# Graph network on one core: 166 regions walked in place of 168, 625 tiles gathered in place of 628, and in the attention output TensorE takes a chunk's product ahead of the next chunk's turn

## The chip, the core and the metric

The kernel runs on one core of a Trainium2 chip. The metric is the device time of one execution in microseconds (us), as the median of several runs. A core has TensorE (PE, matrix products and transposes into PSUM; its weight loads are shown apart as PEld), VectorE (DVE), ScalarE (ACT), GpSimd (POOL) and SyncE (SP). They run at the same time and wait for each other by semaphores. TensorE's clock is granted at one of two levels, 1.2 or 2.4 GHz; the profile shows the mean grant of a stretch as a share of the upper one.

## The reference

`x` holds 5000 nodes of 128 features, `src` and `dst` name the ends of 80000 edges (sorted by `dst`). Four graph layers are added to `x` one after the other:

```python
h = relu(layernorm(x)); x = x + L0(h, edges, edge_attr_128)   # GAT with edge rows, 3 iterations
h = relu(layernorm(x)); x = x + L1(h, src, dst)               # sum of relu(x[src]) by dst, MLP, batch norm
h = relu(layernorm(x)); x = x + L2(h, edges, edge_attr_4)     # 4 steps: typed messages, sums by dst, GRU
h = relu(layernorm(x)); x = x + L3(h, src, dst)               # transformer attention over edges, batch norm, FFN
# in L0, three times:
k, v = x[src] + edge_attr through wk, wv;  alpha = sum(q[dst] * k) / sqrt(32)      # 4 heads
a = exp(alpha - segment_max(alpha, dst));  a = a / segment_sum(a, dst)
att = segment_sum(a * v, dst)
att = layernorm(att @ w_ao.T + b_ao + x)                      # the "attention output"
m = layernorm(gelu(att @ w_int.T) @ w_out.T + att);  h = gru(m, h);  x = layernorm(h)
```

## The kernel before

The edges lie in 625 **tiles** of 128 (one edge per partition), the nodes in 40 **blocks** of 128. Where a tile's edges point into several blocks, it is taken once for each: a **step** is a pair of tile and block. 625 + 40 - 1 = 664 steps are enough for any sorted `dst`. The kernel walks 672, since `STEPS = ROW_C * ROW_K` = 7 x 96; the last eight repeat tile 624 with block 40, which stands behind the nodes. Four steps are a **region** (`GROUP`), four regions a turn of a loop (`REGIONS`), so 168 regions in 42 turns (`LOOPS`). `turns` writes the first and the last turn out and loops over the rest.

The stages, in order:
- Per iteration of L0 (three): a **score pass** (`gat_score_pass`), `gat_softmax`, a **value pass** (`gat_value_pass`), the **attention output** (`attended`), the feed-forward part, the GRU and the norm. In the score pass GpSimd gathers the rows `x[src]`, one indirect DMA of 128 rows a step (`gathers_by_step`, L969, into a ring of four regions); SyncE loads the edge rows (L1369); VectorE makes selection matrices (L991), adds the edge rows (L1421) and forms the scores (L1431 to L1438); TensorE transposes (L1453, L1461) and multiplies (L1473, L1480); ScalarE copies out of PSUM, and SyncE stores the values in HBM (L1376). The value pass reads them back (L1519), GpSimd and VectorE weigh half of a region each (L1529, L1545), and TensorE sums by node block in PSUM (L1578); the number of a block's last region is read from a table (`value_done`).
- L1 has the **mixing pass** (`mixing_pass`) and L2 four **update passes** (`update_pass`). They don't walk steps: each tile is gathered once (`gathers_by_tile`, L986, into a ring of eight regions; 157 regions, `TILE_REGIONS`, the last one with tile 624 and three columns of index 0), and 196 pairs of region and block are summed. SyncE waits for a region's gathers and passes the news on (`relay_landed`, L1084, and L1087 for the last region); VectorE picks a selection three pairs ahead (L1036) and adds the sum of a pair (L1060, behind TensorE's L1074). Near the end the node chunks that are complete are transposed (L1130; L1278 in the mixing pass) and run through the gates between the pairs.
- L3 has the **transformer pass** (`transformer_pass`), again 168 regions of steps with gathers at L969, then attention output, norms and feed-forward.

In `attended` the nodes lie in ten chunks of 512 columns. GpSimd forms the sums with the bias for chunk c (L1960, L1963, once chunk c-2 has been turned); VectorE weighs them (`weigh`, L1970); TensorE transposes (`turn`, L1998); ScalarE copies (L2021); TensorE takes the product with `w_ao` (`project`, L2004); VectorE adds (`finish`, L1975); then TensorE transposes again (L714) for the norm, VectorE takes the statistics (L729), ScalarE scales, TensorE turns back (L722). Each engine's order is written out by hand: VectorE in turn t does `weigh(t)`, `finish(t-1)`, `measure(t-2)`, `scale(t-3)`; TensorE `turn(t)`, `project(t-1)`, `turn_nodes(t-2)`, `turn_back(t-4)`.

## Time and profile before

| | before |
|---|---|
| runs, us | 9507.3, 9508.18, 9516.57; median 9508.18 |
| profiled execution, us | 9523.01 (its span 9521.2) |
| mean granted clock of TensorE | 0.787 |
| busy us: PE / PEld / DVE / ACT / POOL | 6133.9 / 4836.9 / 4478.9 / 2035.6 / 6058.3 |
| instructions | 134262 |

Busy shares are means over stages with different limits, and idle time costs only where the engine is waited for. The first score pass runs from about 173 to 1025 us, its value pass from 1072 to 1274, the attention output to about 1336; the mixing pass starts at 4283, the four update passes at 5171, 6003, 6840 and 7672, the transformer pass at 8557.

### The profile page before, as it was taken

How to read it: one execution, taken by the hardware profiler on the slowest of the kernel's cores; microseconds unless marked ns; L12 is line 12 of the kernel's file. 1: busy time of each engine (PE TensorE's matmuls, PEld its weight loads, DVE VectorE, ACT ScalarE, POOL GpSimd, SP SyncE). 2: the span in 40 equal slices, each digit the busy share in tenths (PEclk: the TensorE clock that was granted, in tenths of full speed). 3: DMA queues.
4: the chain of work that ended last, by engine and by line, in shares of the span. 5: the costliest groups of instructions: out<-in, count | busy, mean ns of one | idle time of the engine just before them, and what ended most of it. 6: DMA issues, size and time to landing. Idle time of an engine off the chain costs nothing. (4 is left out here: it accounts for less than half of the span.)

```text
span 9521.2 us, 134262 instructions
## 1 busy us (share of the span) xinstructions
PE 6133.9 (64%) x31445; PEld 4836.9 (51%) x31446; DVE 4478.9 (47%) x9847; ACT 2035.6 (21%) x4047; POOL 6058.3 (64%) x6482
## 2 busy tenths in 40 slices
PE   4878787887787886874445446544644654476666
PEld 3666655666646665743443444344344434445554
DVE  5555755555845556842224223322422332257776
ACT  2444244444054443160001000000100000021112
POOL 2777435777417775517774777677677767747773
PEclk7999899999889998985556557655855765598888
DMA  3555523555604554602112222222222222233332
GB/s 87 159 159 159 156 79 98 159 159 155 184 11 143 159 159 121 181 23 53 53 53 78 53 52 78 61 53 53 86 53 52 78 61 53 52 97 105 105 105 65
DMA packets 708452, 916.20 MB, mean 96 GB/s; under 512 B 148175, under 2 KB 448091, under 8 KB 708078
## 3 DMA queue, kind: packets, MB, share of 16 engines
q0 software_dynamic: 198368, 429.61, 17.3%
q1 hardware_dynamic: 487108, 441.09, 14.8%
q10 hardware_dynamic: 22730, 42.81, 1.2%
q8 instruction: 83, 1.36, 0.1%
q14 instruction: 163, 1.34, 0.0%
HBM read 702.69 MB, written 210.24 MB: 96 GB/s over the span
## 5 line engine op out<-in xcount | busy, mean ns | idle before, releaser
L986 POOL DMA_INDIRECT states<-table_typed,tile_idx x2512 | 2401.7, 956 | 993.6 <-issue 767.7
L969 POOL DMA_INDIRECT states<-table_x,src_idx x2016 | 1910.3, 948 | 722.4 <-issue 599.5
L1074 PE MATMUL psum<-states,select 128*128 x4480 | 1003.7, 400 | 1118.1 <-DVE t L1060 1037.5
L1074 PEld LDWEIGHTS psum<-states,select 128*128 128x128 f32 x4480 | 893.2, 298 | 1253.9 <-issue 1253.5
L1036 DVE SCALAR_TENSOR_TENSOR select<-dst_all,pair_start,psum 128x512 f32<-128x512 f32 x476 | 355.4, 747 | 1583.8 <-SPq L1084 1323.7
L1473 PE MATMUL psum<-wt,l_scores_mixT 128*128 128x256 f32 x4032 | 992.8, 389 | 38.2 <-issue 35.5
L1074 PE MATMUL psum<-states,l_update_select 128*128 x2688 | 570.8, 385 | 538.3 <-DVE t L1060 538.3
L1480 PE MATMUL psum<-t,l_scores_spread 128*128 x4032 | 586.1, 288 | 443.1 <-DVE score L1438 440.4
L969 POOL DMA_INDIRECT l_pass_ring<-table_kv,src_idx x672 | 642.9, 957 | 297.7 <-issue 204.6
L1473 PEld LDWEIGHTS psum<-wt,l_scores_mixT 128*128 128x128 f32 x4032 | 728.1, 190 | 194.9 <-issue 106.8
L1074 PEld LDWEIGHTS psum<-states,l_update_select 128*128 128x128 f32 x2688 | 510.7, 285 | 611.5 <-issue 611.5
L1421 DVE TENSOR_TENSOR states<-states 128x512 f32<-128x512 f32 x504 | 349.1, 693 | 975.0 <-DMA states<-table_x,src_idx 975.0
L1480 PEld LDWEIGHTS psum<-t,l_scores_spread 128*128 128x128 f32 x4032 | 490.7, 190 | 559.8 <-issue 559.8
L991 DVE TENSOR_TENSOR select<-psum,dst_local 128x512 f32<-128x512 f32 x1008 | 692.4, 687 | 125.9 <-PE psum L1578 48.7
L986 POOL DMA_INDIRECT states<-table_x,tile_idx x628 | 594.0, 946 | 232.8 <-issue 176.2
L1222 ACT COPY t<-psum 128x512 f32<-128x512 f32 x40 | 23.5, 586 | 2793.4 <-PE psum L1130 2793.4
L1529 POOL TENSOR_TENSOR t<-t,score 128x264 f32<-128x264 f32 x504 | 345.2, 688 | 417.3 <-DMA t<-rows_dram 412.6
L1578 PE MATMUL psum<-t,select 128*128 128x132 f32 x4032 | 492.4, 281 | 73.1 <-DVE t L1545 40.5
L1036 DVE SCALAR_TENSOR_TENSOR l_update_select<-dst_all,pair_start,psum 128x512 f32<-128x512 f32 x264 | 197.0, 746 | 717.3 <-SPq L1084 680.0
L1578 PEld LDWEIGHTS psum<-t,select 128*128 128x128 f32 x4032 | 469.0, 192 | 100.6 <-issue 100.6
L1389 ACT COPY l_scores_spread<-psum 128x512 f32<-128x512 f32 x504 | 295.4, 586 | 732.3 <-PE psum L1453 732.3
L1401 ACT COPY w<-psum 128x512 f32<-128x512 f32 x504 | 295.5, 586 | 712.2 <-PE psum L1473 623.6
(414 smaller groups left out, 9618.1 us busy)
## 6 DMA issues: line engine op xcount, KB each, us to landing
rows_dram<-l_scores_values SPq DMA_DIRECT2D x504, 264.0 KB
t<-rows_dram SPq DMA_DIRECT2D x504, 264.0 KB, 3.0
states<-in_edge_attr_dram SPq DMA_DIRECT2D x2016, 64.0 KB
states<-table_typed,tile_idx POOLq DMA_INDIRECT x2512
table_typed<-states ACTq DMA_DIRECT2D x36, 1024.0 KB, 4.5
states<-table_x,src_idx POOLq DMA_INDIRECT x2016
table_x<-select SPq DMA_DIRECT2D x50, 256.0 KB, 2.3
l_pass_ring<-table_kv,src_idx POOLq DMA_INDIRECT x672
```

The lines of the kernel that those rows point to most:

```text
L969: pool.indirect_dma_start(out=ring[:, k % REGIONS, u, :], out_offset=None, in_=table, in_offset=at).then_inc(gathered[k % REGIONS], 16)
L986: pool.indirect_dma_start(out=ring[:, k % TILE_RING, u, :], out_offset=None, in_=table, in_offset=at).then_inc(gathered[k % REGIONS], 16)
L991: eng.tensor_tensor(select[:, r, lo:lo + n, :], numbers.unsqueeze(1).broadcast_to([P, n, P]), dst_local[:, bass.ds(step_of(i, r, lo), n)]. ...
L1036: dve.scalar_tensor_tensor(out=picked(more, k), in0=dst_all[:, bass.ds(column, GROUP)].unsqueeze(2).broadcast_to([P, GROUP, P]), scalar=pa ...
L1074: ins = pe.matmul(psum[:, k % 2, 0:P], picked(more, k)[:, u, :], slots[:, bass.ds(at[u], D)], start=u == 0, stop=u == GROUP - 1)
L1389: act.copy(spread[:, r % 2, :, :], bank4(psum[:, 0, :])).then_inc(p_spread, 1)
L1401: act.copy(in_pairs(key[:, r % 2, :, :]), made(r)[:, :, :, 0:D]).then_inc(p_evacuated, 1)
L1421: dve.tensor_tensor(ring[:, r, :, :], ring[:, r, :, :], attr[:, r, :, :], ALU.add).then_inc(p_mixed, 1)
L1473: ins = pe.matmul(made(r)[:, u // pair, u % pair, :], mixT[:, r % 2, u, :], both, start=True, stop=True)
L1480: ins = pe.matmul(queries[:, u // pair, u % pair, :], spread[:, r % 2, u, :], q, start=True, stop=True)
L1529: pool.tensor_tensor(ring[:, room(half, r), SHARE:, :].rearrange("p u (h e) -> p u h e", h=GAT_HEADS), ring[:, room(half, r), SHARE:, :].r ...
L1578: ins = pe.matmul(to, select[:, r, u, :], ring[:, room(half, r), u, :], start=False, stop=True, skip_group_check=True)
```

## The change

Three edits. (1) The passes over steps walk 166 regions, `EDGE_REGIONS`, in place of 168: the last turn has two regions and the one ahead of it is written out too, `regions_of` and `led` stop at the last region, counts of semaphores follow (`STEP_COUNTS`, `step_landed`), and the eight steps of `score` that are no longer written are set to zero. (2) The last region of the passes over tiles gathers one tile in place of four. (3) In `attended` TensorE's `project(t-1)` stands ahead of `turn(t)`.

```diff
+EDGE_REGIONS = -(-(TILES + BLOCKS - 1) // GROUP)
...
-                    link(dve.tensor_scalar(counts_i[:], psum[0:1, 7, CHUNK - VALUE_BANKS:], float(GROUP - 1), None, ALU.add))
+                    link(dve.tensor_scalar(counts_i[:], psum[0:1, 7, CHUNK - VALUE_BANKS:], float(GROUP - 1), float(EDGE_REGIONS * GROUP),
+                                           ALU.add, ALU.min))
...
             body(0)
-            with eng.Fori(1, LOOPS - 1) as i:
+            with eng.Fori(1, LOOPS - 2) as i:
                 body(i)
+            body(LOOPS - 2)
             body(LOOPS - 1)
...
+        def regions_of(i):
+
+            return range(min(REGIONS, EDGE_REGIONS - i * REGIONS)) if isinstance(i, int) else range(REGIONS)
+
...
-            return None if isinstance(i2, int) and i2 >= LOOPS else (i2, r2)
+            return None if isinstance(i2, int) and i2 * REGIONS + r2 >= EDGE_REGIONS else (i2, r2)
...
-        ROWS = LOOPS * GROUP * 16
-
-        TILE_COUNTS = [len(range(r, TILE_REGIONS, REGIONS)) * GROUP * 16 for r in range(REGIONS)]
...
+        STEP_COUNTS = [len(range(r, EDGE_REGIONS, REGIONS)) * GROUP * 16 for r in range(REGIONS)]
+
+        TILE_COUNTS = [len(range(r, TILES, REGIONS * GROUP)) * 16 for r in range(REGIONS * GROUP)]
+        TILE_COUNTS = [sum(TILE_COUNTS[r * GROUP:(r + 1) * GROUP]) for r in range(REGIONS)]
...
+        def step_landed(i, r, base):
+
+            return base[r] + STEP_COUNTS[r] if isinstance(i, int) and i == LOOPS - 1 else landed(i, base[r])
...
-            for k in range(STEPS // GROUP):
+            for k in range(EDGE_REGIONS):
...
-                for u in range(GROUP):
+                for u in range(min(GROUP, TILES - k * GROUP)):
...
-                sp.wait_ge(gathered[r], landed(TILE_REGIONS // REGIONS, base[r]))
+                sp.wait_ge(gathered[r], base[r] + TILE_COUNTS[r])
...
-                            for r in range(REGIONS):
+                            for r in regions_of(i):
...
+                        dve.memset(score[:, EDGE_REGIONS * GROUP:, :], 0.0)
+
...
-                            dve.wait_ge(gathered[r], landed(i, base[r]))
+                            dve.wait_ge(gathered[r], step_landed(i, r, base))
...
-                        add_blocks(dve, sums, LOOPS - 1, REGIONS - 1, W, blocks_of(dve, LOOPS - 1, REGIONS - 1))
+                        final = (EDGE_REGIONS - 1) // REGIONS, (EDGE_REGIONS - 1) % REGIONS
+                        add_blocks(dve, sums, *final, W, blocks_of(dve, *final))
...
                         for t in range(CHUNKS + 4):
+                            if 1 <= t <= CHUNKS:
+                                project(t - 1)
                             if t < CHUNKS:
                                 turn(t)
-                            if 1 <= t <= CHUNKS:
-                                project(t - 1)
```

The line `for r in regions_of(i)` takes the place of `for r in range(REGIONS)` in every body of the score, value and transformer passes.

TensorE in `attended`, from its start; before (L1998 `turn`, L2004 `project`, L714 `turn_nodes`, L722 `turn_back`):

```order
L1998 MATMUL psum<-ident,w 128x128 x8
L2004 MATMUL psum<-select,wt 128x512
L1998 MATMUL psum<-ident,w 128x128 x4
L2004 MATMUL psum<-select,wt 128x512
L714 MATMUL psum<-ident,t 128x128 x4
L1998 MATMUL psum<-ident,w 128x128 x4
L2004 MATMUL psum<-select,wt 128x512
L714 MATMUL psum<-ident,t 128x128 x4
```

The same place in the changed kernel, whose lines are numbered L2015, L2021, L728 and L736:

```order
L2015 MATMUL psum<-ident,w 128x128 x4
L2021 MATMUL psum<-select,wt 128x512
L2015 MATMUL psum<-ident,w 128x128 x4
L2021 MATMUL psum<-select,wt 128x512
L2015 MATMUL psum<-ident,w 128x128 x4
L728 MATMUL psum<-ident,t 128x128 x4
L2021 MATMUL psum<-select,wt 128x512
L2015 MATMUL psum<-ident,w 128x128 x4
```

The two sets of turning transposes at the start (x8) are parted by the first product, and each later product has moved from behind a set of transposes to ahead of it.

GpSimd at the end of the last update pass and through the transformer pass, before (L986 gathers by tile, L969 by step):

```order
L986 DMA states<-table_typed,tile_idx 128x128 x12
L977 REGISTER_ALU
L986 DMA states<-table_typed,tile_idx 128x128 x4
L93 UNCONDITIONAL_BRANCH
L2346 REGISTER_ALU
L2346 COMPARE_AND_BRANCH
L1607 UNCONDITIONAL_BRANCH
L969 DMA l_pass_ring<-table_kv,src_idx 128x256 x672
```

And in the changed kernel (L1000 and L983):

```order
L1000 DMA states<-table_typed,tile_idx 128x128 x12
L991 REGISTER_ALU
L1000 DMA states<-table_typed,tile_idx 128x128
L94 UNCONDITIONAL_BRANCH
L2363 REGISTER_ALU
L2363 COMPARE_AND_BRANCH
L1623 UNCONDITIONAL_BRANCH
L983 DMA l_pass_ring<-table_kv,src_idx 128x256 x664
```

The last region has one gather where it had four, and the pass over steps has 664 where it had 672. In the score pass the same row counts 664 too.

## Rows read from the trace of the kernel before

**Rows 1.** Windows: us; busy (xcount) of PE, PEld, DVE, ACT, POOL; PEclk; DMA share; GB/s.
```profile
500.00:600.00 100.00, 79.98 (x481) 65.64 (x481) 56.65 (x100) 42.98 (x80) 75.60 (x81) 1.00 0.55 159
...
1100.00:1200.00 100.00, 86.03 (x716) 81.86 (x715) 94.39 (x179) 7.62 (x14) 61.76 (x90) 1.00 0.80 242
...
1273.50:1325.00 51.50, 30.57 (x120) 19.08 (x120) 28.78 (x101) 21.59 (x50) 23.09 (x20) 0.77 0.00 0
```
**Rows 2.** Timeline, first score pass: first and last of 672 gathers, first softmax transposes.
```profile
172.68 0.98 POOL L969 DMA_INDIRECT states<-table_x,src_idx  x1 [89.33 <-POOLq L93]
...
1013.19 0.95 POOL L969 DMA_INDIRECT states<-table_x,src_idx  x1 [0.30 <-issue]
...
1024.95 4.94 PE L1739 MATMUL psum<-ident,score 128*96 128x128 f32 x28 [2.56 <-PEq L93]
```
**Rows 3.** Timeline, engine PE: last two bursts of the first value pass.
```profile
1265.42 3.86 PE L1578 MATMUL psum<-t,select 128*128 128x132 f32 x32 [0.55 <-DVE t L1545]
...
1269.60 3.86 PE L1578 MATMUL psum<-t,select 128*128 128x132 f32 x32 [0.32 <-DVE select L991]
```
**Rows 4.** Timeline, engine POOL: last gather of the transformer pass.
```profile
9403.38 0.95 POOL L969 DMA_INDIRECT l_pass_ring<-table_kv,src_idx  x1 [0.31 <-issue]
```
**Rows 5.** Timeline, end of the fourth update pass.
```profile
8462.83 0.95 POOL L986 DMA_INDIRECT states<-table_typed,tile_idx  x1 [0.30 <-issue]
...
8467.29 1.05 PE L1074 MATMUL psum<-states,select 128*128 x8
...
8469.56 0.75 DVE L1036 SCALAR_TENSOR_TENSOR l_update_select<-dst_all,pair_start,iota_row 128x512 f32<-128x512 f32 x1 [5.01 <-SPq L1087]
...
8470.57 0.66 PE L1130 MATMUL psum<-ident,t 128*128 128x128 f32 x4 [2.23 <-DVE t L1060]
```
**Rows 6.** Timeline: the same transposes in mixing and update passes one to three.
```profile
5072.81 1.12 PE L1278 MATMUL psum<-ident,t 128*128 128x128 f32 x4 [4.28 <-DVE t L1060]
...
5968.85 0.66 PE L1130 MATMUL psum<-ident,t 128*128 128x128 f32 x4 [1.61 <-DVE t L1060]
...
6802.17 0.66 PE L1130 MATMUL psum<-ident,t 128*128 128x128 f32 x4 [1.96 <-DVE t L1060]
...
7637.13 0.66 PE L1130 MATMUL psum<-ident,t 128*128 128x128 f32 x4 [1.73 <-DVE t L1060]
```
**Rows 7.** Timeline, attention output, first iteration: weighing of chunk 1; one whole turn.
```profile
1279.05 1.55 DVE L1970 TENSOR_TENSOR w<-w,l_attention_den 128x512 f32<-128x512 f32 x1 [1.08 <-POOL w L1963]
...
1309.45 0.69 DVE L1970 TENSOR_TENSOR w<-w,l_attention_den 128x512 f32<-128x512 f32 x1
...
1310.20 0.66 PE L1998 MATMUL psum<-ident,w 128*128 128x128 f32 x4 [1.41 <-DVE w L1970]
...
1310.69 1.02 PE L2004 MATMUL psum<-select,wt 128*128 128x512 f32 x2
...
1311.62 0.60 ACT L2021 COPY select<-psum 128x512 f32<-128x512 f32 x1
...
1311.76 0.75 DVE L1975 SCALAR_TENSOR_TENSOR t<-psum,vec,states 128x512 f32<-128x512 f32 x1 [1.61 <-PE psum L2004]
...
1312.10 1.18 POOL L1963 TENSOR_TENSOR w<-w,states 128x512 f32<-128x512 f32 x1
...
1312.42 0.88 DVE L729 BATCH_NORM_STATS2 norm_stat<-psum 128x6 f32<-128x128 f32 x4
...
1313.89 0.69 DVE L1970 TENSOR_TENSOR w<-w,l_attention_den 128x512 f32<-128x512 f32 x1
```
**Rows 8.** Timeline, engine PE, attention output: a turn at the lower clock.
```profile
1319.31 1.11 PE L1998 MATMUL psum<-ident,w 128*128 128x128 f32 x4 [1.40 <-DVE w L1970]
...
1321.92 1.03 PE L714 MATMUL psum<-ident,t 128*128 128x128 f32 x4
```
**Rows 9.** Timeline: GpSimd and VectorE at the head of the attention output.
```profile
1276.35 1.07 POOL L1960 TENSOR_TENSOR w<-states,bv_rows 128x512 f32<-128x512 f32 x1
...
1276.53 1.44 DVE L1970 TENSOR_TENSOR w<-w,l_attention_den 128x512 f32<-128x512 f32 x1
```

More of the change, by code:

```diff
@@ L1381, in _ @@
                         for r in range(REGIONS):
-                            sp.wait_ge(p_out[r], 16 * LOOPS)
+                            sp.wait_ge(p_out[r], 16 * len(range(r, EDGE_REGIONS, REGIONS)))
                     @b.scalar
@@ L1395, in body @@
                         def body(i):
-                            for r in range(REGIONS):
+                            for r in regions_of(i):
                                 if nxt := led(i, r, 1):
@@ L1423, in body @@
                         def body(i):
-                            for r in range(REGIONS):
+                            for r in regions_of(i):
                                 if nxt := led(i, r):
@@ L1464, in body @@
                         def body(i):
-                            for r in range(REGIONS):
+                            for r in regions_of(i):
                                 j = region_of(i, r)
@@ L1516, in body @@
                     def body(a, i, half):
-                        for r in range(REGIONS):
+                        for r in regions_of(i):
                             at_least(sp, p_summed, region_of(i, r) - (ROOMS - 1))
@@ L1525, in body @@
                     def body(a, i, half):
-                        for r in range(REGIONS):
+                        for r in regions_of(i):
                             weights = score[:, bass.ds(step_of(i, r), GROUP), :]
@@ L1538, in body @@
                     def body(a, i, half):
-                        for r in range(REGIONS):
+                        for r in regions_of(i):
                             j = region_of(i, r)
@@ L1568, in body @@
                         plan = by_step(pe, value_row, region_of(i, 0) * (GROUP + 1), REGIONS * (GROUP + 1), BANKS_USED * CHUNK)
-                        for r in range(REGIONS):
+                        for r in regions_of(i):
                             j = region_of(i, r)
@@ L1617, in body @@
                         def body(i):
-                            for r in range(REGIONS):
+                            for r in regions_of(i):
                                 act.wait_ge(p_scored, region_of(i, r) + 1)
@@ L1634, in body @@
                             blocks = blocks_behind(dve, i)
-                            for r in range(REGIONS):
+                            for r in regions_of(i):
                                 j = region_of(i, r)
@@ L1638, in body @@
                                 dve.wait_ge(p_projected, j + 1)
-                                dve.wait_ge(gathered[r], landed(i, base[r]))
+                                dve.wait_ge(gathered[r], step_landed(i, r, base))
                                 dve.tensor_tensor(prod, ring[:, r, :, 0:D], bank4(q_bank(r)), ALU.mult).then_inc(p_multiplied, 1)
@@ L1692, in body @@
                         def body(i):
-                            for r in range(REGIONS):
+                            for r in regions_of(i):
                                 if nxt := led(i, r, 1):
@@ L2317, in program @@
         with nc.Fori(0, GAT_ITERS) as it:
-            gat_score_pass("l0_scores", [it * ROWS] * REGIONS)
+            gat_score_pass("l0_scores", [it * n for n in STEP_COUNTS])
             gat_softmax("l0_softmax")
@@ L2329, in program @@
         node_rows("l1_norm", resT, hT, LN_EPS, plus=xT)
-        mixing_pass("l1_sums", table_x[:], [GAT_ITERS * ROWS] * REGIONS, hT, t1, wt[:, GIN1, :], wcol("1_b1"))
+        mixing_pass("l1_sums", table_x[:], [GAT_ITERS * n for n in STEP_COUNTS], hT, t1, wt[:, GIN1, :], wcol("1_b1"))
         batch_norm("l1_second", t1, wcol("1_gamma"), wcol("1_beta"), residual=resT, weight=wt[:, GIN2, :], bias=wcol("1_b2"))
@@ L2348, in program @@
                 update_pass(f"l2_update{k}", table_typed[k].ap().rearrange("n (t f) -> (n t) f", f=D),
-                            [GAT_ITERS * ROWS + n * (1 + k) + it * (2 * n) for n in TILE_COUNTS], hT,
+                            [GAT_ITERS * m + n * (1 + k) + it * (2 * n) for m, n in zip(STEP_COUNTS, TILE_COUNTS)], hT,
                             parts_of(wt, GGIH, 3), parts_of(wt, GGHH, 3), gate_bias[:, 1, :], wcol("2_b_ih", 2), wcol("2_b_hh", 2),
@@ L2355, in program @@
         projected_rows("l3_norm", resT, xT, LN_EPS, w3[:, 0:3, :].rearrange("p a b -> p (a b)"), 3 * D, table_kv, plus=hT, query_width=D)
-        transformer_pass("l3_pass", [GAT_ITERS * ROWS + (1 + L2_STEPS) * n for n in TILE_COUNTS])
+        transformer_pass("l3_pass", [GAT_ITERS * m + (1 + L2_STEPS) * n for m, n in zip(STEP_COUNTS, TILE_COUNTS)])
         from_rows("l3_attention", t1, heads=L3_HEADS, eps=1e-6, weight=w3[:, 3, :], bias=wcol("3_bo"), residual=xT)
```

1 line of the change is left out of this document (added).

## The prediction, made before the changed kernel had run

> **What bounds the kernel now.** I read the windows first, 100 us apart over the span. In a score pass GpSimd is busy 75.6 us of 100 with 81 instructions, and the clock granted to TensorE is 1.00 (its upper level, 2.4 GHz) [rows 1]. The timeline says what the other quarter is: a gather takes 0.95 us and the next one starts 0.30 us later, with "issue" as the reason. From the first gather to the last of the first score pass there are 671 intervals in 840.51 us, 1.253 us each [rows 2]. So a region (4 gathers) costs 5.01 us, and the reader is to see that nothing but GpSimd's own issue stands before the gathers. The same rhythm fills the transformer pass and the mixing and update passes [rows 4, 5]. In a value pass no gather runs; VectorE is busy 94 us of 100 and the DMA engines 0.80 [rows 1], and TensorE sums four regions in bursts that start 4.18 us apart [rows 3]. The attention output is bound by none of its engines: TensorE 30.6, VectorE 28.8, ScalarE 21.6 and GpSimd 23.1 us of 51.5 [rows 1]. It is a round trip between VectorE and TensorE.
>
> **Two regions fewer in each score pass.** POOL issues 664 gathers in place of 672. The last gather starts at 1013.19 and the softmax begins at 1024.95 [rows 2]: those 11.8 us are the drain of the last regions through VectorE, TensorE, ScalarE and the store of the values, and they hang on the last region, whichever it is. 8 x 1.253 = 10.0 us less per pass, **30.1 us** in three. I cost four things at nothing. The turn that is now written out ahead of the last one runs the same instructions as in the loop. The wait values are constants. The limit on the counts is one more scalar of the same instruction. The zeroing of 8 steps of `score` stands ahead of VectorE's wait for ScalarE's copies and for region 0, whose four gathers alone take 5 us; without that cover it costs less than the 0.69 us of a 512-column operation [rows 7], 2 us in three passes.
>
> **Two regions fewer in each value pass.** The last turn has two regions, so TensorE's last burst of 3.86 us [rows 3] is half as long: 1.93 us, and ScalarE drains the last bank behind it as before. **5.8 us** in three passes. The bounds are close: 2.1 us per pass by the burst's spacing, and nothing if the last burst has to wait for its rows from HBM.
>
> **Two regions fewer in the transformer pass.** The gathers go on to its end at the same distance [rows 4]: **10.0 us**.
>
> **Three gathers fewer in the last region of the mixing pass and of four update passes.** The last region now lands after one gather, 3 x 1.25 = 3.8 us earlier at least. But how much of it arrives? At the end of the fourth update pass VectorE has waited 5.01 us for that region when it makes its selection at 8469.56 [rows 5]. The addition behind it needs also the sum of an earlier pair, which TensorE starts at 8467.29 and ends at 8468.34. Without the wait for the region that sum becomes the last thing to come. TensorE's transposes, which wait for the addition, stand idle 2.23 us before 8470.57; when they follow a sum directly this handover needs about 0.35 us (0.28 of addition and the signal; 8469.56 to 8470.57 is 1.01 with the 0.7 us selection ahead of it). So 1.9 us of the 3.8 arrive. The other update passes have 1.61, 1.96 and 1.73 us in the same place [rows 6], less 0.35 each: together **6.2 us** for the four. In the mixing pass there is no gate work between, and the idle time is 4.28 us: **3.9 us**. The bounds: nothing below what the transposes show, at most the whole wait of 5.01 us in each of five passes, 25 us.
>
> **Attention output: the product ahead of the turn.** In a turn t at the upper clock [rows 7]: the weighing of chunk t at 1309.45, TensorE's transposes of it at 1310.20 (0.75 later), the product of chunk t-1 at 1310.69 (0.49), VectorE's addition to it at 1311.76 (1.07), the statistics of chunk t-2 at 1312.42 (0.66), the next weighing at 1313.89 (1.47): 4.44 us. The product is in the middle of the chain although its input is long ready: ScalarE's copy for the next product ends at 1312.22, 2.77 us after the weighing. After the change the product of chunk t runs from about 2.8 to 3.8 us after weighing t, while VectorE does statistics; it is over before the next weighing. Queued behind its wait are the transposes of the next turn; as the copy comes first, nothing there is late. What is left of the chain is 0.75 + 0.49 + 0.65 (transposes of chunk t-2, as long as the 0.66 of the others) + 1.47 = 3.36 us. The next limit is GpSimd. Its second operation starts 2.65 us after the weighing and ends at 3.83 [rows 7], later than 3.36. At the head of the pass a weighing beside a GpSimd operation took 1.44 in place of 0.69 us: it started at 1276.53 and ended 0.55 us after GpSimd's had ended at 1277.42 [rows 9]. A weighing that waits in this way ends at 3.83 + 0.55 = 4.38, not 3.36 + 0.69 = 4.05: the turn becomes 3.69 us.
>
> The Trainium skill (SBUF — State Buffer, Who interferes with whom) says that a VectorE operation with two inputs in SBUF and a GpSimd operation that reads SBUF exclude each other for a whole instruction. By that rule the turn is 3.69 us and by a chain without it 3.36; the trace agrees with the rule at this one place.
>
> At the lower clock (1.2 GHz; the same transposes take 1.11 us) transposes and product take 2.61 us [rows 8], so the old chain is 0.75 + 2.61 + 1.03 + 1.5 = 5.9 us. In the new one TensorE itself is full: 2.61 + 2 x 0.86 for the two other sets of transposes (1.03 to 1.11 us each [rows 8], of which some 0.2 overlap with what follows) = 4.33 us. The seven turns from 1279.05 to 1313.89 took 4.98 us each [rows 7], so about 0.37 of them are slow ones (granted clock 0.77 over the stretch [rows 1]). New mean: 0.63 x 3.69 + 0.37 x 4.33 = 3.93; 1.05 us less, nine turns, three iterations: **28 us**. The bounds are nothing (another engine takes the slack) and 27 x (4.98 - 3.36) = 44 us.
>
> **Sum.** 30.1 + 5.8 + 10.0 + 6.2 + 3.9 + 28 = 84 us. The profiled execution took 9523.0 us (span 9521.2 and 1.8 around it) and becomes 9439; it lay 14.8 us above the median of the runs, 9508.2, and the same 84 us from that give **9424 us**.
>
> **Rivals.**
> A, the forecast: chance 0.62.
> B, the reordering gives nothing, because GpSimd, VectorE and ScalarE meet in every turn: 84 - 28 = 56 us, 9452. For it speaks the 1.44 us weighing [rows 9]; against it, that no engine is busy more than 0.6 of the stretch [rows 1]. Chance 0.17.
> C, everything gives its upper bound: the weighing isn't held (44) and the whole wait for the last region goes (25): 30 + 6 + 10 + 25 + 44 = 115 us, 9393. Against it stands TensorE's sum at 8468.34 [rows 5]. Chance 0.08 for most of it.
> D, the dropped regions were hidden in part, because the end of a score pass hangs on the edge rows or on the store of the values and not on the gathers: half of the 46 us of regions, 9447 with the rest. Against it: the gathers show no wait but issue [rows 2]. Chance 0.08.
> E, slower. The written-out turn makes code of two loops longer, and leaving the loop stalls every engine for fetching it. The nearest row is TensorE's 2.56 us before the first work of a new block [rows 2]: four passes of it would be 10 us, 9434, still faster. It decides only from 84 / 4 = 21 us per pass, more than the 15 us that three regions of gathers run ahead, so it would also have to stop the gathers. Chance 0.02 for slower, 0.03 for a gain eaten down to within 0.2%.
>
 The trace of before shows no stall there that reaches the gathers, since their mean of 1.253 us [rows 2] takes in the loops' end.
>
> **Numbers.** A change under 0.2% (19 us) can't be told from none here. A, B, C and D are faster by more than that: 0.95; same 0.03; slower 0.02. The range reaches to B and D with some room above, and half way to C: 9402 to 9460. A alone would be 9412 to 9436.
>
> **What would show it.** Right, if the gathers of a score pass number 664 and the softmax still starts 11.8 us after the last; if the selection at the end of an update pass no longer waits 5 us and the transposes' idle time is near 0.35; if weighings in the attention output stand 3.7 us apart at the upper clock. Wrong, if the drain has grown, if weighings last over 1 us throughout or their distance stays at 4.4, or if TensorE pauses where the loops end.

## The result and the profile after

The changed kernel takes 9420.97 us (median of 4 runs, 9416.41 to 9422.73); the kernel before took 9507.74 beside it (4 runs). The ratio is 0.9905, 95% interval 0.9893 to 0.9916: 86.8 us less, where I had said 84. The profiled execution took 9419.24 us.

The page of the changed kernel: its span, and the first row of busy times.

```profile
span 9417.4 us, 133392 instructions
...
PE 6101.1 (65%) x31213; PEld 4812.4 (51%) x31214; DVE 4442.9 (47%) x9788; ACT 2021.3 (21%) x4017; POOL 6001.4 (64%) x6429
```

The same three stretches as [rows 1] in windows (busy time of PE, PEld, DVE, ACT, POOL, granted clock, DMA share, GB/s); the third is the attention output, which now starts 12 us earlier.

```profile
500.00:600.00 100.00, 80.65 (x484) 65.88 (x482) 56.91 (x101) 42.99 (x80) 75.59 (x80) 1.00 0.54 160
...
1100.00:1200.00 100.00, 86.79 (x723) 82.60 (x722) 92.67 (x181) 7.03 (x13) 62.78 (x90) 1.00 0.82 242
...
1262.00:1313.00 51.00, 29.59 (x141) 17.78 (x142) 34.06 (x123) 30.88 (x71) 23.26 (x20) 0.89 0.00 1
```

The middle of a score pass and of a value pass is what it was. In the attention output VectorE is busy 34.1 us of 51 instead of 28.8 of 51.5, since its turns stand closer and the window reaches further past the last weighing (15 us, where it was 6). TensorE was granted 0.89 of its upper clock (2.4 GHz) instead of 0.77 in this first iteration.

The timeline of the first score pass: first and last gather, first transposes of the softmax. Then TensorE's last burst of the first value pass, and the last gather of the transformer pass.

```profile
172.72 0.97 POOL L983 DMA_INDIRECT states<-table_x,src_idx  x1 [89.79 <-POOLq L94]
...
1001.91 0.95 POOL L983 DMA_INDIRECT states<-table_x,src_idx  x1 [0.30 <-issue]
...
1014.85 1.50 PE L1756 MATMUL psum<-ident,score 128*96 128x128 f32 x6 [2.80 <-PEq L94]
...
1258.83 2.06 PE L1594 MATMUL psum<-t,select 128*128 128x132 f32 x16 [0.42 <-issue]
...
9298.96 0.95 POOL L983 DMA_INDIRECT l_pass_ring<-table_kv,src_idx  x1 [0.30 <-issue]
```

664 gathers start within 829.19 us, 1.2507 us apart ([rows 2]: 672 in 840.51, 1.2526 apart). The softmax starts 12.9 us after the last one; it was 11.8. The last burst of the value pass has 16 sums in 2.06 us, where [rows 3] shows 32 in 3.86.

The end of the fourth update pass: last gather (GpSimd), selection for the last region (VectorE), TensorE's last sum ahead of the transposes and the transposes.

```profile
8369.23 0.94 POOL L1000 DMA_INDIRECT states<-table_typed,tile_idx  x1 [0.30 <-issue]
...
8374.75 0.75 DVE L1050 SCALAR_TENSOR_TENSOR l_update_select<-dst_all,pair_start,iota_row 128x512 f32<-128x512 f32 x1
...
8377.57 1.05 PE L1088 MATMUL psum<-states,select 128*128 x8
...
8378.46 0.60 PE L1144 MATMUL psum<-ident,t 128*128 128x128 f32 x4
```

In [rows 5] the selection had waited 5.01 us and the transposes 2.23. Now neither row has an idle time: the region is there before VectorE asks for it, and TensorE goes from its sum straight into the transposes.

A turn of the attention output at the upper clock, sorted by start time.

```profile
1288.19 1.07 POOL L1977 TENSOR_TENSOR w<-states,bv_rows 128x512 f32<-128x512 f32 x1 [1.41 <-PE psum L2015]
...
1289.34 1.18 POOL L1980 TENSOR_TENSOR w<-w,states 128x512 f32<-128x512 f32 x1
...
1289.62 1.05 PE L2021 MATMUL psum<-select,wt 128*128 128x512 f32 x2
...
1289.98 0.56 DVE L755 SCALAR_TENSOR_TENSOR norm_offset<-norm_moment,norm_std 128x4 f32<-128x4 f32 x1
...
1290.46 0.68 DVE L1987 TENSOR_TENSOR w<-w,l_attention_den 128x512 f32<-128x512 f32 x1
...
1291.06 0.74 DVE L1992 SCALAR_TENSOR_TENSOR t<-psum,vec,states 128x512 f32<-128x512 f32 x1
...
1291.20 0.66 PE L2015 MATMUL psum<-ident,w 128*128 128x128 f32 x4 [0.54 <-DVE w L1987]
...
1291.69 0.60 PE L728 MATMUL psum<-ident,t 128*128 128x128 f32 x4
...
1292.33 0.89 DVE L743 BATCH_NORM_STATS2 norm_stat<-psum 128x6 f32<-128x128 f32 x4 [0.53 <-PE psum L728]
...
1294.20 0.68 DVE L1987 TENSOR_TENSOR w<-w,l_attention_den 128x512 f32<-128x512 f32 x1
```

The product (L2021) stands ahead of the weighing now, and the weighings are 3.74 us apart (1290.46, 1294.20), against 4.44 in [rows 7] and 3.69 in the prediction. But look at the row above the weighing. The norm's offset (L755), 512 numbers in all, takes 0.56 us. It ends at 1290.54, and GpSimd's second operation ends at 1290.52. The weighing itself takes its bare 0.68. The hold that I had placed on the weighing has fallen on the small operation in front of it. The experiments on this are the second half of the next section.

### The profile page after: what moved, and what is told of

The parts are those of the page before. It is cut to its first block and busy times, and to the rows that moved or that the text cites. A ratio compares the mean times of both kernels' runs of the same rounds, so it can differ in the third digit from the quotient of the medians.

```text
span 9417.4 us, 133392 instructions
## 1 busy us (share of the span) xinstructions
PE 6101.1 (65%) x31213; PEld 4812.4 (51%) x31214; DVE 4442.9 (47%) x9788; ACT 2021.3 (21%) x4017; POOL 6001.4 (64%) x6429
## 3 DMA queue, kind: packets, MB, share of 16 engines
q1 hardware_dynamic: 481924, 436.27, 14.8%
## 5 line engine op out<-in xcount | busy, mean ns | idle before, releaser
L1000 POOL DMA_INDIRECT states<-table_typed,tile_idx x2500 | 2384.5, 954 | 993.5 <-issue 761.7
L983 POOL DMA_INDIRECT states<-table_x,src_idx x1992 | 1883.9, 946 | 713.7 <-issue 587.0
L983 POOL DMA_INDIRECT l_pass_ring<-table_kv,src_idx x664 | 634.1, 955 | 295.6 <-issue 201.6
L1000 POOL DMA_INDIRECT states<-table_x,tile_idx x625 | 589.8, 944 | 231.6 <-issue 178.0
L1594 PE MATMUL psum<-t,select 128*128 128x132 f32 x3984 | 486.3, 281 | 72.1 <-DVE t L1561 40.8
```

Of the source, the lines that this page charges most:

```text
L983: pool.indirect_dma_start(out=ring[:, k % REGIONS, u, :], out_offset=None, in_=table, in_offset=at).then_inc(gathered[k % REGIONS], 16)
L1000: pool.indirect_dma_start(out=ring[:, k % TILE_RING, u, :], out_offset=None, in_=table, in_offset=at).then_inc(gathered[k % REGIONS], 16)
L1594: ins = pe.matmul(to, select[:, r, u, :], ring[:, room(half, r), u, :], start=False, stop=True, skip_group_check=True)
```

## Where the time came from, by the two traces

Both traces give marks on GpSimd: its gathers, and its first operation of each block. In us, sums over all passes of a kind:

| stretch | before | after | difference | predicted |
|---|---|---|---|---|
| three score passes, first to last gather | 2521.5 | 2487.3 | -34.2 | -30.1 |
| last gather to the value pass | 187.2 | 191.1 | +3.9 | 0 |
| three value passes | 593.9 | 588.3 | -5.6 | -5.8 |
| attention output and the block behind it | 648.8 | 614.3 | -34.5 | -28 |
| five passes by tile, first to last gather | 3946.9 | 3920.4 | -26.5 | |
| what lies behind them until the next gathers | 326.7 | 331.3 | +4.6 | |
| the two rows together | | | -21.9 | -10.1 |
| transformer pass, first to last gather | 846.5 | 835.1 | -11.4 | -10.0 |

That is 103.7 us, as much as the two profiled executions differ (9523.0 and 9419.2), but 17 more than the medians. The surplus has a place. All gather stretches together lost 72.1 us; 47 gathers fewer at 1.255 us are 59.0. The other 13.1 us is 5,781 remaining gathers that stand 0.0023 us closer on average. That is a property of the execution and not of the change: two kernels with 166 regions have 1.2526 and 1.2525 us in the first pass again (the regions alone, and the first try against the hold, both below), and the profiled execution of before had been 14.8 us above its median. Taken off, the parts are 26 (score passes with their drains), 6, 34, 14 (tiles) and 10 us: 90 for the 87 measured.

## The experiments

The experiments are built on either kernel with one addition, a register operation behind each table entry that a later wait uses. Two kernels that hold only that addition are the controls.

```
 regs = [eng.alloc_register(...) for _ in range(n)]
 eng.load(regs, table[0:1, bass.ds(first, n)])
+for k in waited:
+    held = eng.alloc_register(...)
+    eng.reg_alu(held, regs[k], max(bottom, 1), ALU.max)
+    regs[k] = held
```

> The kernel before, with one register operation (the larger of the entry and 1) behind every table entry that a later wait uses; nothing else is changed. It is the control of the kernels that are built on the kernel before. The operation stands on GpSimd's path of issues in six passes of gathers by tile, some 145 times in each, and on VectorE, TensorE and ScalarE beside them, where gathers set the pace. If it is as cheap as the gaps of 0.02 to 0.05 us between gathers allow, the five passes by tile grow by less than 1 us each and the time stays within 0.1% of 9507.7 us. If each costs GpSimd 0.05 us in the open, the passes grow by 7 us each, some 36 us in all. Whatever it is, the experiments are read against this control and not against the kernel before.

> The changed kernel with the same register operations. It is the control of the kernels that are built on the changed kernel. Against the first control it should be 87 us faster (the two kernels without these operations stood at 9420.97 and 9507.74 us), so 0.990 to 0.992 of it, whatever the operations cost.

Measured: 11389.54 us and 11293.24 us, beside 11371.47 for the kernel before, ratios 1.0016 (1.0007 to 1.0026) and 0.9922 (0.9908 to 0.9935). This chip ran every kernel 20% slower than the others did, the kernel before too, so its times are compared with one another only. A window of the first control in a score pass, to be held against [rows 1], and a row of the waits there:

```profile
500.00:600.00 100.00, 70.09 (x364) 59.80 (x363) 41.00 (x73) 31.47 (x60) 58.24 (x61) 0.86 0.41 120
...
DVE states L1436 <- issue: 51.7, 14, 6.7
```

GpSimd issues 61 gathers in 100 us instead of 81. VectorE waited there 14 times for nothing that the profile shows, up to 6.7 us each and 51.7 us in all. Why this chip does that stayed open. The second control was run again on an ordinary chip.

> The second control once more, as the base of the three kernels beside it. Its ratio to the kernel before should again be near 0.992, and in its trace the turn of the attention output 3.75 us, with the small operation of VectorE (the norm's offset, 0.16 us by itself) held to 0.55 us.

Measured: 9442.74 us beside 9512.56, ratio 0.9927 (0.9913 to 0.9940). The addition costs 0.16 to 0.22%, 15 to 21 us, more than expected. The gathers kept their distance, so it isn't on GpSimd's path of issues. By the marks of the table above, most of it lies in the value passes: they take 199.7 to 200.3 us each in this run, where the changed kernel had 195.7 to 196.5, so 12 us in three. In every kernel with the addition a value pass takes 199.7 to 202.6 us. There the addition stands four times in each turn of TensorE's loop; that it costs on that path is argued from the place and not tested. Where the other 3 to 9 us lie wasn't settled. What follows is read against the controls, and by marks in the traces.

### The reordering alone

```
 for t in range(CHUNKS + 4):
+    if 1 <= t <= CHUNKS:
+        project(t - 1)
     if t < CHUNKS:
         turn(t)
-    if 1 <= t <= CHUNKS:
-        project(t - 1)
```

> The first control with the reordering of TensorE in the attention output alone; 168 regions and 628 gathered tiles as before. My forecast: attended falls by 28 us over three executions; the trace of the changed kernel showed 34 us less between the start of that block and the next norm, so 28 to 35 us below the first control, and no other mark moves. Rival (the reordering gives nothing, since GpSimd's two operations and the transposes close the turn): within 5 us of the first control, the 34 us belonging to the shorter score accumulators or to another clock behind shorter passes.

Measured: 11354.18 us against 11389.54 of the first control, 35 us less (ratios to the kernel before 0.9981 and 1.0016). Two consecutive weighings late in the third iteration, first control and then this kernel:

```profile
4919.45 0.68 DVE L1976 TENSOR_TENSOR w<-w,l_attention_den 128x512 f32<-128x512 f32 x1
...
4923.89 0.68 DVE L1976 TENSOR_TENSOR w<-w,l_attention_den 128x512 f32<-128x512 f32 x1
```

```profile
4877.79 0.68 DVE L1976 TENSOR_TENSOR w<-w,l_attention_den 128x512 f32<-128x512 f32 x1
...
4881.54 0.68 DVE L1976 TENSOR_TENSOR w<-w,l_attention_den 128x512 f32<-128x512 f32 x1
```

4.44 us became 3.75, and from VectorE's reciprocal at the head of the attention output to GpSimd's first operation of the block behind it the three iterations lost 10.6, 9.9 and 10.5 us: 31 us in all. Rival B, by which the reordering gives nothing, is out.

### The regions alone

The changed kernel with TensorE's old order and all 628 tiles.

> The changed kernel with 166 regions, but with TensorE's old order in the attention output and with all 628 tiles gathered. By my sum: score passes 30.1, value passes 5.8 and the transformer's pass 10.0 us, so 46 us below the first control; each pass by step loses the eight gathers of two regions, 8 times 1.25 us. By the ledger of the two traces where GpSimd's gathers set the pace (34.2, 5.6 and 11.4 us) it is 51. Rival D (what is dropped was partly hidden, since something other than the gathers ends a pass): 23 us. On a chip where the passes by step run at 1120 us instead of 840, a region costs more than four gathers and the two dropped ones should give 3 times 2 times 6.7 us in the score passes, 40 us, and 55 to 60 in all.

Measured: 9491.06 us beside 9523.72, ratio 0.9964 (0.9950 to 0.9978); with the controls' 0.16 to 0.22% taken off, 48 to 54 us. In its trace the score passes take 830.50, 831.12 and 830.81 us from first to last gather, 29.1 us less than before in sum, and the transformer pass 836.67, 9.8 less. In this execution the gathers stand as far apart as before (1.2526 us in the first pass), so here the price of dropped regions can be read directly: 9.7 us per score pass on average and 9.8 in the transformer pass, for two regions each, where the prediction had 10.0. The value passes take 600.66 us in sum; the kernel with real rows below, on the same chip and with the addition too, has 605.93: 5.3 us less for a predicted 5.8. Rival D, half of it hidden, is out.

### The tiles alone

```
-for u in range(GROUP):
+for u in range(min(GROUP, TILES - k * GROUP)):
```

> The first control with the last region of a pass by tile gathered for its one real tile (625 gathers instead of 628) and nothing else. By my sum of the prediction: the mixing pass and four update passes together lose 10 us (3.9 and 4 times 1.5), of a bound of 25. By the ledger of the two traces they lost 22 us (7.3 and 14.6), of which the three gathers themselves are 3 times 1.25 us in each of five passes, 18.8 us. Theory of the issue: 18 to 22 us below the first control, the landing of the last region now some 1.8 us behind its gather. Rival (part of the 22 us came from elsewhere, as the regions' count or the clock): 10 us or less.

Measured: 11380.68 us, 9 us below the first control, on the slow chip, where the eleven runs of this kernel lie up to 40 us apart. The intervals of the two ratios (0.9996 to 1.0015 and 1.0007 to 1.0026) overlap, so this run doesn't tell 10 from 20 us. Nor does its trace: the five passes and what lies behind them take 4922 us, and the other three kernels on this chip have 4938 and 4935 with 628 gathers and 4939 with 625. So no run on record isolates the three gathers; what they bring is counted from the marks of the kernels on the other chips, in the point by point below.

### Where the last region's lateness came from

```
-at = bass.IndirectOffsetOnAxis(ap=tile_idx[:, k * GROUP + u:k * GROUP + u + 1], axis=0)
+n = k * GROUP + u if k * GROUP + u < TILES else k * GROUP + u - GROUP
+at = bass.IndirectOffsetOnAxis(ap=tile_idx[:, n:n + 1], axis=0)
```

> The first control, in which the three padding tiles of the last region of a pass by tile fetch the rows of three real tiles instead of row 0 128 times each; their sums are multiplied by zero as before. It asks why the last region landed 5.8 us behind its last gather where others took 1.8. Theory of the equal rows (128 fetches of one row go to one place of the memory and are served one behind the other): the last region lands within 2 us of its last gather, and each of the five passes by tile ends 3 to 4 us sooner. Rival (the end of the queue itself is late, whatever is fetched): the selection still waits 5 us and nothing moves. My terms for the tiles (3.9 and 6.2 us) left this out; the ledger had 7.3 and 14.6.

Measured: 9528.53 us beside 9523.72 (ratio 1.0003, 0.9994 to 1.0012). The last gather of the fourth update pass and the selection for its region:

```profile
8466.17 0.94 POOL L988 DMA_INDIRECT states<-table_typed,tile_idx  x1 [0.30 <-issue]
...
8469.78 0.75 DVE L1042 SCALAR_TENSOR_TENSOR l_update_select<-dst_all,pair_start,iota_row 128x512 f32<-128x512 f32 x1 [0.74 <-SPq L1093]
```

The selection comes 3.6 us after the last gather and has waited 0.74 us; in [rows 5] it came 6.7 us after it and had waited 5.01. In the mixing pass it comes 2.7 us after it, not 4.3. By the DMA packets of the gathers' queue, the last one ends 2.1 to 4.3 us after the last gather in the five passes, where it had been 3.7 to 6.2. So three gathers that fetch one and the same row 128 times each land 1.5 to 3.1 us later than three that fetch different rows. Around the end of the gathers the packets took 0.27 to 0.42 us each on average in the kernel before, and 0.12 to 0.13 here. In the update passes 1 MB of other transfers runs beside the last gathers, but in both kernels alike. This half of the theory holds.

The other half, that each pass then ends 3 to 4 us sooner, comes out in part. From the last gather to the next pass the five stretches are 320.2 us in sum. The kernel before had 326.7, but it lacks the addition; the two kernels that have the addition, this chip and the equal rows (regions alone, written-out turn) had 329.0 and 330.9. That is 9 to 11 us less, some 2 us a pass. The ratio says the same less sharply: 1.0003 against the first control's 1.0016 is 12 us less, though the two intervals overlap a little. TensorE's own sums are next, as the prediction had argued from 8467.29.

### The written-out turn alone

```
 with eng.Fori(1, LOOPS - 2) as i:      # was LOOPS - 1
     body(i)
+body(LOOPS - 2)
 body(LOOPS - 1)
```

> The first control with one more turn of each loop of regions written out behind the loop (the turn before the last), still 168 regions, 628 tiles and the old order. Forecast: nothing, within 3 us of the first control (0.03%). Rival E (the code behind the loop's exit is fetched late, once more per pass): 2.56 us by the nearest row in each of the four passes by step, 10 us more, and over 21 us in each pass if it were to turn the change into a loss. In the trace the stretch from the last loop turn's gathers to the end of a pass would be longer by that.

Measured: 9535.98 us beside 9523.72 (ratio 1.0012, 1.0003 to 1.0021), less than the addition costs by itself, so in total time the turn can't be seen. In the trace it can. From the last gather of a score pass to the softmax it takes 13.8, 13.6 and 13.6 us; before 11.8, 11.7 and 11.9. Two of its rows, the softmax's first transposes in the first pass and, near the end of the second, the addition for a region that came late:

```profile
1025.51 0.84 PE L1746 MATMUL psum<-ident,score 128*96 128x128 f32 x3 [4.55 <-PEq L93]
...
2364.00 0.69 DVE L1427 TENSOR_TENSOR states<-states 128x512 f32<-128x512 f32 x1 [4.22 <-DMA states<-table_x,src_idx]
```

In the first pass TensorE waits 4.55 us at the block's start where [rows 2] shows 2.56. In the second that wait is 2.94, but VectorE has waited 4.22 us for a gathered region; the waits of this kind before were 2.4 us at most in the last 20 us of that pass. On the ordinary chips the distance was 11.6 to 11.9 us in the six score passes of kernels without the written-out turn; in the 21 passes of the seven kernels with it and 166 regions it was 11.6 to 13.9, 12.4 on average. So the written-out turn has a price, as rival E said: 0.6 us per pass on average (1.9 with 168 regions), where its own estimate was 2.56. The prediction had put it at nothing. That it is a price for fetching code isn't shown. Why it shows in some passes and not in others wasn't found.

### The hold

The changed kernel's turn is 3.74 us though VectorE still waits 0.5 us in it (from 1291.80 to 1292.33, for the transposes of L728). The first try was to take that wait away.

```
 if 1 <= t <= CHUNKS:
     project(t - 1)
+if 2 <= t < CHUNKS + 2:
+    pe.wait_ge(a_done, t - 1)
+    turn_nodes(pe, t1, t - 2, first=FIRST)
 if t < CHUNKS:
     turn(t)
-if 2 <= t < CHUNKS + 2:
-    pe.wait_ge(a_done, t - 1)
-    turn_nodes(pe, t1, t - 2, first=FIRST)
```

> The changed kernel with one more move of the same kind: in the attention output TensorE takes the transposes for the statistics of chunk t-2, which are ready since the turn before, ahead of chunk t's turn instead of behind it. In the trace of the changed kernel VectorE waits 0.52 us for them in each turn of 3.75 us. If that wait goes and nothing takes its place, a turn falls to 3.35 us or less (that is what the last turn without GpSimd took), 0.4 us in each of 8 turns in 3 executions: 10 us below the second control. Rival (ScalarE, with 3.00 us of work and 0.80 us of waits for VectorE's small operations in a turn, is the next bound, or the transposes for the chunk now come later and GpSimd with them): within 3 us of the second control.

Measured: 9450.04 us beside 9523.72, ratio 0.9921 (0.9907 to 0.9935), the second control's. A turn of it:

```profile
1292.25 0.60 PE L728 MATMUL psum<-ident,t 128*128 128x128 f32 x4
...
1292.95 0.66 PE L2021 MATMUL psum<-ident,w 128*128 128x128 f32 x4
...
1293.48 0.87 DVE L743 BATCH_NORM_STATS2 norm_stat<-psum 128x6 f32<-128x128 f32 x4
...
1293.68 1.07 POOL L1983 TENSOR_TENSOR w<-states,bv_rows 128x512 f32<-128x512 f32 x1 [1.41 <-PE psum L2021]
...
1294.84 1.18 POOL L1986 TENSOR_TENSOR w<-w,states 128x512 f32<-128x512 f32 x1
...
1294.86 1.17 DVE L755 SCALAR_TENSOR_TENSOR norm_offset<-norm_moment,norm_std 128x4 f32<-128x4 f32 x1
...
1295.96 0.68 DVE L1993 TENSOR_TENSOR w<-w,l_attention_den 128x512 f32<-128x512 f32 x1
```

VectorE no longer waits: its statistics (L743) follow the addition at once. The turn is 3.75 us nevertheless, and the offset (L755) takes 1.17 us instead of 0.56. It starts at 1294.86 and ends at 1296.03; GpSimd's addition ends at 1296.02. All the time that the move had freed went into the hold. So there is a ring: GpSimd's two operations 2.34 us (1293.68 to 1296.02), the weighing that can only end after them 0.67 until TensorE's transposes start, and the transposes, on which GpSimd waits for its next chunk, 0.74 with the signal. That is 3.75 us, however early VectorE comes to the offset. The forecast of 10 us less was wrong; the rival had the outcome, not the cause.

Two theories for the ring were put against each other. Three rooms in place of two (`third` is a new tile; GpSimd waits for `a_turned` one chunk further back):

```
+def sums(c):
+    return pair[:, c % S, :, :] if c % S < V else third[:]
-at_least(pool, a_turned, c - (V - 1))
+at_least(pool, a_turned, c - (S - 1))      # S = V + 1
```

> The second control with three rooms instead of two for GpSimd's sums in the attention output, so that GpSimd runs a chunk further ahead of VectorE's weighing. The run before it showed that with VectorE's wait gone a turn is still 3.75 us, and that is GpSimd's two operations (2.33), the weighing (0.75) and the transposes (0.67) end to end. Two theories for what closes this ring. If it is the held operation (VectorE can't end an operation with both inputs in SBUF while GpSimd's runs, and GpSimd starts at the end of a turn's transposes), a third room changes nothing: 3.75 us, within 3 us of the control. If it is the rooms (a weighing waits for sums that came late), the ring opens: 3.35 us, 10 us less.

and behind that one more wait for GpSimd, which makes it start at the end of a weighing:

```
 at_least(pool, a_turned, c - (S - 1))
+at_least(pool, a_rows, c - 1)
```

> The kernel with the third room, where GpSimd also waits for the weighing of two chunks before, and so starts at the end of each weighing and no longer at the end of the transposes, 0.8 us earlier against VectorE's work. By the held operation's theory GpSimd's 2.33 us then end before the norm's offset begins (0.27 us before it by the rows of the changed kernel), the offset takes 0.16 us again and a turn 3.35 us: 0.4 us less in 8 turns of 3 executions, 10 us below the control. By the theory of the rooms it is as the third room alone or slower by the added wait.

Measured: the third room 9446.25 us, ratio 0.9928 (0.9915 to 0.9942), the control's 9442.74 within its spread. With the added wait 9434.12 us, ratio 0.9917 (0.9903 to 0.9930): by the medians 8.6 us less than the control. Third room, then the added wait:

```profile
1294.11 1.18 POOL L1991 TENSOR_TENSOR w<-w,states 128x512 f32<-128x512 f32 x1
...
1294.75 0.56 DVE L755 SCALAR_TENSOR_TENSOR norm_offset<-norm_moment,norm_std 128x4 f32<-128x4 f32 x1
...
1295.23 0.68 DVE L1998 TENSOR_TENSOR w<-w,l_attention_den 128x512 f32<-128x512 f32 x1
```

```profile
1292.52 0.68 DVE L1999 TENSOR_TENSOR w<-w,l_attention_den 128x512 f32<-128x512 f32 x1
...
1294.51 1.18 POOL L1992 TENSOR_TENSOR l_attention_third<-l_attention_third,states 128x512 f32<-128x512 f32 x1
...
1295.79 0.16 DVE L755 SCALAR_TENSOR_TENSOR norm_offset<-norm_moment,norm_std 128x4 f32<-128x4 f32 x1
...
1295.87 0.68 DVE L1999 TENSOR_TENSOR w<-w,l_attention_den 128x512 f32<-128x512 f32 x1
```

In the first the offset is held to 0.56 us, until GpSimd's end at 1295.29, and the weighings stay 3.75 us apart: the rooms are not what closes the ring. In the second GpSimd is done at 1295.69, 0.10 us before the offset begins. The offset takes 0.16 us and the weighings stand 3.35 us apart (1292.52, 1295.87), in the last six intervals of the second iteration as well (3.32 to 3.36). In the three iterations together the attention output and the block behind it take 606.9 us, where the control has 612.4 and the third room alone 612.0. So the added wait shortened this stretch by 5 us. For the whole kernel the gain is less sure: its five runs (9432.55 to 9435.38) lie below all five of the third room, but one run of the control took 9426.36, and the intervals of the ratios overlap.

> The kernel with the third room and the start behind the weighing, and TensorE's transposes for the statistics first. VectorE's own work of a turn is then 3.0 us in a row and ScalarE's 3.0 us. By the held operation's theory GpSimd ends some 0.3 us into where the offset would begin, so a turn is 3.3 us, about what the late start's removal gives alone, and the time 10 to 12 us below the control. If holds don't matter it would reach 3.05 us, 17 us below.

Measured: 9434.47 us, ratio 0.9913 (0.9899 to 0.9926), 8.3 us below the control, where 10 to 12 or 17 were expected. The offset and the next weighings in its trace:

```profile
1292.23 0.68 DVE L1999 TENSOR_TENSOR w<-w,l_attention_den 128x512 f32<-128x512 f32 x1
...
1295.16 0.25 DVE L755 SCALAR_TENSOR_TENSOR norm_offset<-norm_moment,norm_std 128x4 f32<-128x4 f32 x1
...
1295.33 0.68 DVE L1999 TENSOR_TENSOR l_attention_third<-l_attention_third,l_attention_den 128x512 f32<-128x512 f32 x1
```

The turn is 3.10 us, close to the 3.05 that stood for "holds don't matter" and below my 3.3: GpSimd, too, starts earlier within the turn, and the hold that is left is 0.09 us (0.25 instead of 0.16). Between the first and the last weighing the three iterations take 4.9 us less than with the old order, but the totals of the two kernels are equal, their runs overlapping (9425.13 to 9435.46 and 9432.55 to 9435.38). All these kernels carry the addition of the controls, and none of their ratios lies below the changed kernel's 0.9905. That the wait would help the changed kernel itself is inferred from the control and was not run.

## Why the prediction was right, point by point

- **Score passes.** The price of a region is GpSimd's issue: 29.1 us measured with regions alone, 30.1 predicted. The step "the written-out turn at nothing" was off, but by little. The stretch from the last gathers to the value passes grew by 3.9 us in the changed kernel's trace (187.2 to 191.1); over the seven kernels with 166 regions it is 187.6 to 191.1, 189.1 on average, where before and the one with real rows have 187.2 and 188.6. So 1 to 2 of the 3.9 us are the change's.
- **Value passes.** 5.6 us for 5.8, and 5.3 with regions alone. The last burst of TensorE is half as long, 1.8 us less.
- **Transformer pass.** 9.8 us with regions alone for 10.0.
- **Passes by tile.** Predicted 10.1, found 10 to 14. The pair of traces has 14 (18.8 for the 15 gathers less 4.6 given back behind them). The kernels with the addition give less: behind the gathers two of them with 628 gathers have 329.0 and 330.9 us, five with 625 have 335.2 to 340.9, 338.9 on average, so 9 are given back and 10 are left. I had measured at the transposes of [rows 5, 6] and taken their idle time as what arrives. In the pair it came out there: no wait at the selection (0.37 us in the mixing pass), no idle time at the transposes. In the mixing pass the transposes come 9.0 us after the first gather of the last region before and 4.5 after, 4.5 us for my 3.9; in the update passes 11.1, 11.4, 10.9 and 11.5 before and 9.3, 9.1, 11.8 and 9.2 after, 5.4 us in sum for my 6.2 (6.1 before rounding). That is 9.9 at these marks for 10.1. It is partly luck: in the 20 update passes of the five kernels with the addition the transposes come 9.4 to 13.2 us after that gather, 11.4 on average, so one pair of traces doesn't fix this term within a few us.
- **Attention output.** Predicted 28, found 34.5 by the traces and 31 by the reordering alone. The turn at the upper clock: 3.74 for 3.69. The mean over nine turns: 4.71 before and 3.81 after, so 0.90 us each and 24 us, not 1.05 and 28; I had taken the mean before, 4.98, from seven turns that hold the slow ones. The rest came behind the last weighing, 171.5 us per iteration before and 168.0 after, which I hadn't counted. In the reordering alone the 31 us divide into 27.4 between first and last weighing and 3.6 behind (169.3 against 170.5 per iteration). So the term for the turns was right, a part behind them was missing, and some 6 of the 10 us that the pair shows there are not the reordering's. A part of those is the execution's: in five other kernels with the old order this stretch is 169.6 to 170.6 us per iteration, below the 171.5 of before.
- **The hold.** The 3.69 rested on one weighing that ran 0.55 us past GpSimd's end [rows 9]. The mechanism is the one that bound the turn, but the operation that is held is the one before, 0.16 us long by itself, and it ends 0.02 us after GpSimd's end. So the sum of the prediction, a held weighing that ends at 4.38 us, was not what happened; that it gives 3.69 us for the 3.74 measured is luck. The Trainium skill (SBUF — State Buffer, Who interferes with whom) says that an operation of VectorE with two inputs in SBUF is blocked by one of GpSimd that reads SBUF, for the whole instruction. The traces agree, for the smallest such operation too: in the changed kernel and four of those built on it, 65 offsets were held, and each ended 0.02 or 0.03 us after GpSimd's operation. The same section says that VectorE's operations with one input in SBUF don't contend, outside of modes that use both ports. The traces agree there as well: the addition from PSUM took 0.75 us beside GpSimd in [rows 7] (L1975 at 1311.76, GpSimd at 1312.10) and 0.74 to 0.75 us where GpSimd was idle, and each of the statistics' four parts took 0.28 us with GpSimd busy and with GpSimd idle.
- **Against the rivals.** B and D fell with one run each. C had the weighing not held, which came out, and the turn at 3.36 us, which didn't, since the hold sat elsewhere. E's price exists, at a tenth of the 21 us per pass that would have mattered, or less.

## What to carry to other kernels

Where an engine only issues (here 1.25 us per gather, with nothing to wait for) and its last issue sets the end of the pass, work that is dropped pays in full: 9.7 us for two regions, where eight gathers are 10.0. Where other engines set the end, a part is given back: 5 to 9 of the 18.8 us in the passes by tile. Padding whose fetches all go to one row lands late besides. Where a loop goes round between engines, a step can be moved out of the chain and the chain then closes through another resource: look for an operation that takes longer than its size allows, and at what ends when it ends. Here that was another engine's hold; one more buffer didn't help, and starting the holder at another time did, by an added wait.

## What the runs showed of the hardware

- An operation of VectorE with both inputs in SBUF, 128 x 4 numbers, took 0.16 us by itself, 0.56 us in the changed kernel and 1.17 us with the statistics moved forward, each time up to 0.02 us past the end of GpSimd's operation.
- 384 fetches of one row landed 1.5 to 3.1 us later than as many of different rows; a packet took 0.27 to 0.42 us on average, not 0.12 to 0.13.
- The distance of gathers differs between executions by 0.2% (1.2507 and 1.2526 us), which made 13 us of the 104 between the two profiled ones.
- One chip ran all kernels 20% slower, with pauses of up to 6.7 us on its engines that no record explains, at nearly the same busy times (VectorE 4498 us against 4479 us before).
